# A fourth sine product moved from GpSimd to VectorE, with a new periodic order, in a software-pipelined transformer kernel

## The chip, the cores and the metric

The kernel runs on one core of a Trainium2 chip. The metric is device time in microseconds of one execution. The kernel before took 1717.99 us, the median of three runs that lay between 1716.4 and 1719.74 us.

## The reference

Two stages. First a small cross attention between `x` and `ctx` (16 batch rows of 128 tokens by 128 features). Then a six-layer network over the same 16 rows, each layer a local attention and a gated feed-forward part. The second stage takes nearly all the time:

```python
def attn_layer(x, Wqkv, qs, ksc, Wo):            # x is shift_tokens(x), 16 heads of 64
    q, k, v = split(x @ Wqkv)                    # 128 -> 3 x 1024
    q = l2norm(q) * qs; k = l2norm(k) * ksc
    q = q*cos*scale + rotate_half(q)*sin*scale   # the cosine product plus the sine product
    k = k*cos/scale + rotate_half(k)*sin/scale
    out = local_attention(q, k, v)               # windows of 32, look back one window
    return out @ Wo
def ffn_layer(x, g, bln, W1, b1, W2, b2):
    a, gate = split((layernorm(x)*g + bln) @ W1 + b1)
    return a * gelu(gate) @ W2 + b2
for i in range(6):
    x = attn_layer(shift_tokens(x), ...) + x
    x = ffn_layer(shift_tokens(x), ...) + x
```

## The kernel before, in words

One step n is one batch row in one layer; there are N = 96 of them (6 layers by 16 rows, layers outermost). A row's next layer is 16 steps later, so the steps in flight are independent, and the kernel is software-pipelined: each engine runs one loop, and iteration `it` of it works on steps it, it-1, it-2, ... at once. The number behind an operation is its lag: `scores(0, 1)` in iteration `it` works on step it-1. The order of the operations within an iteration is written out by hand for each engine (`step`, one for each of TensorE = PE, VectorE = DVE, ScalarE = ACT, GpSimd = POOL), and the engines meet only through semaphores. An engine's instructions start in order, so a waiting one holds back all that is behind it. `LAST` is the greatest lag: the loop has N + LAST iterations, the first and last of which hold only part of the work. SyncE (SP) issues the DMAs in an order of its own.

What a step does, with the lag it has before: transpose x (`turn_x`), cast it into two parts (`x_parts`, `x_rest`); four chunks of q and k of 512 columns each, by three matmuls each (`chunk`, lines 987 to 989); for each chunk the squares (ACT, line 538) and their sums by head (DVE `squares`, line 781), the cosine product (DVE `straight`, line 790) and the sine product with the halves of each head swapped. The sine product of chunks 0 to 2 is made by DVE out of PSUM (`swapped`, line 799). That of chunk 3 goes another way: ACT copies the raw chunk out of PSUM (`raw_copy`, line 544), and POOL makes the product (`swapped`, line 382). POOL adds the two products (`add`, line 390) and multiplies by the inverse norm (`normalise`, line 405); PE transposes the result (`turn_qk`, line 994, tile `u`), ACT copies it (`queries`, `keys`). Then scores (lines 1027, 1037), maxima, exponentials, `row_sums`, `divide` (POOL, line 412), `turn_p` (PE, line 994, tile `P`), `p_out` (ACT, line 594), a DMA of the turned weights into block form (`weights_of`, line 325, tile `Pbd`), and the weighted sums (`values`, line 1059), which also read the values moved by one window (`shifted_values`, line 331, tile `vs`). Then `project_out` (line 1071), `residual`, `moments` and `normal` (layer norm; ACT's `deviation`, line 609, lies between the last two), `turn_normal`, two products `up` with the next weights (342 columns), `bias`, `gelu` with two table loads, `gated`, `turn_h` (line 1100), `down` (line 1110), `feed_back`.

In the first 5 layers the weights of the next layer are split into two parts, one block in every second iteration: by ACT (`split_high`) and POOL (`split_low`, line 365). So every second iteration up to about step 80 carries one more instruction on each of the two.

The eight PSUM banks are each shared by two to four kinds of tiles (`BANK_USERS`); before PE writes a bank it waits for all readers of what stood there (`freed`, `FREED`).

Of the kernel before, what the change touches and what calls it, by code (L numbers as in the profile page):

```python
# [6 lines left out]
N = L * NB  # L7
HEADS, DH, WINDOW = 16, 64, 32
# [17 lines left out]
LAST = 4  # L26
SPLIT_LAG = 0
FINISH_AT = [N, N + 1, N + 2, N - 1 + 4]
SWAP_IN_SBUF = (3,)
# [7 lines left out]
def program(nc, x, ctxT, Wqkv, Wo, W1, b1, W2, b2, by_feature, every_token, shape_consts, out):  # L37
# [11 lines left out]
    with es:  # L49
# [43 lines left out]
        raw = sb("raw", [128, 512])  # L93
# [43 lines left out]
        def sems(name, n):  # L137
# [24 lines left out]
        xsh_ready, raw_ready, lv_done, rstd_ready, gelu_done, hT_ready, xfh_done, high_ready = (  # L162
            sem(s) for s in ("xsh_ready", "raw_ready", "lv_done", "rstd_ready", "gelu_done", "hT_ready", "xfh_done",
                             "high_ready"))
        ACT_SEMS = (sq_done + v_ready + q_ready + k_ready + exp_done + PT_ready + OT_ready + ln_done + rn_ready
                    + [xsh_ready, raw_ready, lv_done, rstd_ready, gelu_done, hT_ready, xfh_done, high_ready])
# [6 lines left out]
        xf_read = gv_full[0]  # L173
# [15 lines left out]
        def pipeline(eng, step):  # L189
# [15 lines left out]
            for it in range(tail, N + LAST):  # L205
                peeled(it)

        FREED = {"chunk": ((0, 0, 0, 0), lambda k: [sq_done[k], rot_done[k], raw_ready if k in SWAP_IN_SBUF else t2_done[k]]),
# [3 lines left out]
                 "values": ((2, 3), lambda k: [OT_ready[k]]), "up": ((4, 3), lambda k: [gv_out[k]]),  # L212
                 "Wo": ((3,), lambda k: [res_done]), "xs": ((3,), lambda k: [xh_ready]),
                 "xhT": ((3,), lambda k: [xf_done]), "turn_h": ((4,), lambda k: [hT_ready]),
                 "down": ((4,), lambda k: [h_ready]), "xT": ((0,), lambda k: [xs_split])}
        BANK_USERS = [
            [("turn_qk", 1), ("chunk", 2), ("up", 1)],
            [("xT", 0), ("Wo", 0), ("turn_p", 0), ("xhT", 0)],
            [("v", 0), ("chunk", 3)],
            [("turn_qk", 0), ("chunk", 1), ("scores", 1)],  # L220
            [("chunk", 0), ("turn_qk", 2), ("v", 1)],
            [("xs", 0), ("values", 0)],
            [("values", 1), ("scores", 0), ("turn_p", 1)],
            [("up", 0), ("turn_qk", 3), ("turn_h", 0), ("down", 0)]]
# [54 lines left out]
        def _(sp):  # L279
# [77 lines left out]
        def _(pool):  # L357
# [10 lines left out]
            def step(it, par, on, splitting):  # L368
# [7 lines left out]

                def swapped(c, lag):
                    n = it - lag
                    pool.wait_ge(raw_ready, n_(n) + 1)
                    pool.wait_ge(add_done[(c + 2) % 4], n_(n) + (c >= 2))  # L380
                    pool.sem_inc(wait_met, 1)
                    nc.gpsimd.tensor_tensor(halves(t2[:, c % 2]), halves(raw[:])[:, :, ::-1, :],
                                            TS[:, layer(n), c % 2].broadcast_to([128, HC, DH]).rearrange(
                                                "p h (a d) -> p h a d", a=2), ALU.mult).then_inc(t2_done[c], 1)
# [40 lines left out]
                if on(1):  # L425
                    normalise(1, 1)
                if on(0):
                    copy_x(0)
                if on(1):
                    add(2, 1)  # L430
                    swapped(3, 1)
                    bound_norms(1, 1)
                if splitting and (par + SPLIT_LAG) % 2 == 1:
                    split_low()
                if on(1):
                    add(3, 1)
                    normalise(2, 1)
                    normalise(3, 1)
                if on(2):
                    divide(0, 2)  # L440
                if on(4):
                    gated(4)
                if on(2):
                    divide(1, 2)
                if on(0):
                    add(1, 0)
                    bound_norms(0, 0)
                    add(0, 0)
                    normalise(0, 0)
# [773 lines left out]
```

## Time and profile before

| | |
|---|---|
| median of three runs | 1717.99 us |
| the profiled execution's own time | 1719.63 us |
| its span | 1717.8 us |
| busy PE / DVE / ACT / POOL | 1641.1 / 1467.8 / 1541.2 / 1403.3 us (96 / 85 / 90 / 82%) |
| granted TensorE clock, mean | 0.985 |

Busy time of an engine is the union of its instructions' times. A matmul's recorded end overlaps the next one's start, so a PE that is busy all the time may still lose a few tenths of a microsecond between two starts; that has to be read from the distance of starts. In the chain of waits each piece is the time by which it moved the end forward, so pieces of one engine can be added.

### The profile page before, as it was taken

To read this page: it belongs to the slowest core of one execution; us is meant where nothing else is said; L and a number is where in the kernel's file an instruction comes from. 1 tells how busy PE (TensorE), PEld (TensorE's weight loads), DVE (VectorE), ACT (ScalarE), POOL (GpSimd) and SP (SyncE) were. 2 spreads that over 40 slices of the span, in tenths; PEclk is the share of its full clock that TensorE was granted. 3 is DMA by queue.
4 is the path that set the end of the run, shared out by engine and by line. 5 is a ranking of instruction groups with operands and counts; after the bars stand their busy time and mean duration, and the time that the engine had idled before them with its cause. 6 is when DMAs were issued, how large, how long until landed. Compare 5 with 4: busy or idle time off the path is not lost.

```text
span 1717.8 us, 64013 instructions
## 1 busy us (share of the span) xinstructions
PE 1641.1 (96%) x20016; PEld 1390.2 (81%) x20016; DVE 1467.8 (85%) x3219; ACT 1541.2 (90%) x3285; POOL 1403.3 (82%) x1502
## 2 busy tenths in 40 slices
PE   4489999999999999999999999999999999999996
PEld 2368888888888888888888888888888888888885
DVE  4578888888888888888888888888889889888884
ACT  3379999999999999999999999999999999999995
POOL 1388888888888888888888888888888888888882
PEclk8699999999999999999999999999999999999999
DMA  5012322122322222222222322222232212222122
GB/s 140 23 38 66 87 61 70 49 76 54 88 58 66 63 55 75 76 67 55 69 61 58 75 73 70 54 69 57 61 91 57 64 44 64 50 57 57 49 64 59
DMA packets 71323, 110.42 MB, mean 64 GB/s; under 512 B 9716, under 2 KB 36472, under 8 KB 71288
## 3 DMA queue, kind: packets, MB, share of 16 engines
q1 hardware_dynamic: 71288, 110.01, 25.4%
q8 instruction: 15, 0.25, 0.1%
q14 instruction: 20, 0.16, 0.0%
HBM read 20.85 MB, written 1.05 MB: 13 GB/s over the span
## 4 chain that ended last, share of the span: by engine, by line
PE 42%; ACT 18%; issue 17%; DVE 8%; POOL 7%; ACTq 1%; POOLq 1%; DVEq 1%; DMA 1%; SPq 0%
PE bank L1059 7%; PE bank L994 7%; PE bank L987 6%; PE bank L989 5%; PE bank L988 5%; PE bank L1037 5%; POOL u L390 3%; ACT L620 3%; ACT kT L575 3%; POOL P L412 2%; PE bank L1110 2%; PE bank L1071 2%; ACT qbd L567 2%; ACT L623 2%; ACT P L588 2%
## 5 line engine op out<-in xcount | busy, mean ns | idle before, releaser
L390 POOL TENSOR_TENSOR u<-u,t 128x512 f32<-128x512 f32 x384 | 493.6, 1285 | 22.2 <-DVE u L790 21.6
L405 POOL TENSOR_TENSOR u<-u,rn 128x512 f32<-128x512 f32 x384 | 393.1, 1045 | 85.6 <-ACT rn L557 80.0
L987 PE MATMUL bank<-Wl,xsh 128*128 (+1 forms) x576 | 270.2, 469 | 3.5 <-issue 2.0
L790 DVE TENSOR_TENSOR u<-bank,TC 128x512 f32<-128x512 f32 x384 | 260.8, 679 | 3.4 <-ACT sq L538 3.4
L781 DVE TENSOR_REDUCE ss<-sq 128x8 f32<-128x512 f32 x384 | 259.9, 677 | 3.7 <-ACT sq L538 0.7
L1037 PEld LDWEIGHTS bank<-kT,qbd 128*64 128x64 f32 x6144 | 195.2, 138 | 61.2 <-issue 61.2
L538 ACT ACTIVATE sq<-bank 128x512 f32<-128x512 f32 x384 | 230.3, 600 | 15.4 <-PE bank L989 6.0
L567 ACT COPY qbd<-bank 64x512 f32<-64x512 f32 x384 | 222.9, 581 | 11.1 <-PE bank L994 7.7
L989 PE MATMUL bank<-Wh,xsh 128*128 (+1 forms) x576 | 228.9, 397 | 0.0
L988 PE MATMUL bank<-Wh,xsl 128*128 (+1 forms) x576 | 226.9, 394 | 0.0
L994 PE MATMUL bank<-shape_constants,u 128*128 128x128 f32 x1536 | 225.1, 278 | 0.0
L1037 PE MATMUL bank<-kT,qbd 128*64 128x64 f32 (+1 forms) x6144 | 221.7, 225 | 0.5 <-ACT kT L575 0.4
L799 DVE TENSOR_TENSOR t<-bank,TS 128x512 f32<-128x512 f32 x288 | 197.0, 684 | 18.6 <-issue 8.5
L412 POOL TENSOR_TENSOR P<-P,rs 128x512 f32<-128x512 f32 x192 | 200.9, 1047 | 10.3 <-DVE rs L820 10.3
L1059 PE MATMUL bank<-Pbd,vs 128*64 128x64 f32 x3072 | 198.8, 228 | 2.6 <-DMA Pbd<-PT 2.6
L994 PEld LDWEIGHTS bank<-shape_constants,u 128*128 128x128 f32 x1536 | 177.5, 141 | 26.3 <-issue 0.2
L1071 PEld LDWEIGHTS bank<-WB,OT 128*128 128x128 f32 x1536 | 186.1, 191 | 10.8 <-issue 2.7
L1059 PE MATMUL bank<-Pbd,v 128*64 128x64 f32 x3072 | 189.5, 222 | 0.0
L1071 PE MATMUL bank<-WB,OT 128*128 (+1 forms) x1536 | 187.1, 274 | 2.3 <-ACT OT L600 2.3
L1059 PEld LDWEIGHTS bank<-Pbd,vs 128*64 128x64 f32 x3072 | 154.8, 137 | 31.2 <-issue 16.8
L1059 PEld LDWEIGHTS bank<-Pbd,v 128*64 128x64 f32 x3072 | 155.8, 138 | 0.0
L399 POOL TENSOR_SCALAR ssc<-ss 128x16 f32<-128x16 f32 x192 | 47.6, 248 | 109.9 <-DVE ss L781 109.8
(118 smaller groups left out, 3862.6 us busy)
## 6 DMA issues: line engine op xcount, KB each, us to landing
Pbd<-PT SPq DMA_DIRECT2D x384, 128.0 KB, 2.3
vs<-v SPq DMA_DIRECT2D x96, 384.0 KB, 3.3
Wraw<-in_L_ffn_Wqkv_dram SPq DMA_DIRECT2D x72, 117.5 KB, 2.2
WB<-in_L_ffn_Wo_dram SPq DMA_DIRECT2D x6, 512.0 KB
WB<-in_L_ffn_b_dram SPq DMA_DIRECT2D x6, 341.0 KB
Wraw<-in_L_ffn_W_dram SPq DMA_DIRECT2D x12, 116.0 KB, 2.3
H<-in_x_dram SPq DMA_DIRECT2D x2, 512.0 KB, 5.6
v<-in_ctx_dram SPq DMA_DIRECT2D x2, 512.0 KB, 6.9
```

The lines of the kernel that those rows point to most:

```text
L390: nc.gpsimd.tensor_tensor(u[:, slot, c], u[:, slot, c], t2[:, c % 2], ALU.add).then_inc(add_done[c], 1)
L405: nc.gpsimd.tensor_tensor(by_head(u[:, slot, c]), by_head(u[:, slot, c]), spread(rn[:, slot, HC * c:HC * c + HC], HC, DH), ALU.mult).then_ ...
L567: i = nc.scalar.copy(qbd[r, s, :, :, e], bank_of("turn_qk", 2 * s)[r].rearrange("p (t w i) -> p t w i", t=4, w=4))
L781: nc.vector.tensor_reduce(ss[:, slot, HC * c:HC * c + HC], by_head(sq[:, c % 2]), AX, ALU.add).then_inc(ss_done[c], 1)
L790: nc.vector.tensor_tensor(by_head(u[:, slot, c]), by_head(bank_of("chunk", c)[:]), TC[:, layer(n), c % 2].broadcast_to([128, HC, DH]), ALU ...
L987: nc.tensor.matmul(out, xh_, Wl[:, w], start=True, stop=False)
L988: nc.tensor.matmul(out, xl_, Wh[:, w], start=False, stop=False)
L989: nc.tensor.matmul(out, xh_, Wh[:, w], start=False, stop=True).then_inc(done, 1)
L994: i = nc.tensor.transpose(bank[:, 128 * t:128 * t + 128], src(t), ident[:])
L1037: i = nc.tensor.matmul(out[64 * w2:64 * w2 + 64, at + (32 if w == 0 else 0):at + 64], qbd[:, s, t, w].rearrange("p e i -> p (e i)"), kT[:, ...
L1059: i = nc.tensor.matmul(tokens[64 * e:64 * e + 64, :, w2], (vs, v)[w2][:, slot, head:head + DH], Pbd[:, :, s, t, 64 * w2 + 32 * e:64 * w2 + ...
L1071: i = nc.tensor.matmul(bank_of("Wo")[:, 0:D], OT[:, k // 4, k % 4], weights(n, WO_AT + k * D, D), start=(k == 0), stop=(k == INNER // 128 ...
```

## The change

The sine product of chunk 3 is made by DVE like the other three. `raw_copy`, the tile `raw`, its semaphore, and POOL's `swapped` are gone, and so is the wait of `straight(3)` for the raw copy. The order of all engines within an iteration is written anew, with other lags for some operations: `values(0)` moves from lag 2 to 3; `deviation`, `normal`, `turn_normal`, `affine`, `upper_x`, `lower_x`, `up(1)` and `bias(1)` from 3 to 4; `gated`, `turn_h`, `h_out`, `down` and `feed_back` from 4 to 5; `minus_maxima(0)` and `exp` from 1 to 2; `normalise(1)` from 1 to 0; `shifted_values` from 2 to 1. `LAST` becomes 5. The banks are shared out anew.

```diff
-LAST = 4
+LAST = 5
-FINISH_AT = [N, N + 1, N + 2, N - 1 + 4]
-SWAP_IN_SBUF = (3,)
+FINISH_AT = [N, N + 1, N + 2, N - 1 + 5]
...
-        FREED = {"chunk": ((0, 0, 0, 0), lambda k: [sq_done[k], rot_done[k], raw_ready if k in SWAP_IN_SBUF else t2_done[k]]),
+        FREED = {"chunk": ((0, 0, 0, 0), lambda k: [sq_done[k], rot_done[k], t2_done[k]]),
...
-            [("turn_qk", 1), ("chunk", 2), ("up", 1)],
-            [("xT", 0), ("Wo", 0), ("turn_p", 0), ("xhT", 0)],
...
+            [("values", 1), ("xhT", 0), ("turn_qk", 3), ("Wo", 0), ("up", 1)],
+            [("turn_qk", 1), ("v", 0), ("turn_p", 0)],
...
+            [("xT", 0), ("chunk", 0), ("chunk", 3)]]
...
                 if 0 <= it - 2 < N:
-                    shifted_values(it - 2)
-                if 0 <= it - 2 < N:
                     weights_of(it - 2, 0)
+                if 0 <= it - 1 < N:
+                    shifted_values(it - 1)
                 if 0 <= it - 2 < N:
                     weights_of(it - 2, 1)
...
-                def swapped(c, lag):
-                    n = it - lag
-                    pool.wait_ge(raw_ready, n_(n) + 1)
-                    pool.wait_ge(add_done[(c + 2) % 4], n_(n) + (c >= 2))
-                    pool.sem_inc(wait_met, 1)
-                    nc.gpsimd.tensor_tensor(halves(t2[:, c % 2]), halves(raw[:])[:, :, ::-1, :],
...
-                def raw_copy(c, lag):
-                    n = it - lag
-                    act.wait_ge(ch_full[c], n_(n) + 1)
-                    act.wait_ge(t2_done[c], n_(n))
-                    nc.scalar.copy(raw[:], bank_of("chunk", c)[:]).then_inc(raw_ready, 1)
...
                 def straight(c, lag):
                     n, slot = it - lag, (par + lag) % 2
                     dve.wait_ge(sq_done[c], n_(n) + 1)
-                    if c in SWAP_IN_SBUF:
-                        dve.wait_ge(raw_ready, n_(n) + 1)
```

How the orders of an iteration differ is read from the built programs. TensorE around the transposes of the attention weights (`P`), before:

```order
L994 MATMUL bank_4<-shape_constants,u 128x128 x4
L994 MATMUL bank_7<-shape_constants,u 128x128 x4
L1079 MATMUL bank_5<-H,shape_constants 128x64
L994 MATMUL bank_1<-shape_constants,P 128x128 x4
L987 MATMUL bank_0<-Wl,xsh 128x512
L988 MATMUL bank_0<-Wh,xsl 128x512
L989 MATMUL bank_0<-Wh,xsh 128x512
```

and now (line 972 is the transpose, 1049 `project_out`, 965 to 967 a product, 1005 the start of `scores`):

```order
L972 MATMUL bank_6<-shape_constants,u 128x128 x4
L1049 MATMUL bank_0<-WB,OT 128x128 x8
L972 MATMUL bank_1<-shape_constants,P 128x128 x4
L965 MATMUL bank_3<-Wl,xfh 128x342
L966 MATMUL bank_3<-Wh,xfl 128x342
L967 MATMUL bank_3<-Wh,xfh 128x342
L972 MATMUL bank_6<-shape_constants,P 128x128 x4
L1005 MATMUL bank_4<-maskb,identb 128x512
```

`turn_p(0)` stood right behind `shift`; now it stands behind `project_out`, in the last third of the iteration, and the values that it leads to are the second operation on TensorE in the next one.

VectorE in the last part of an iteration, before (tile `t2` is the sine product, `u` the cosine product):

```order
L849 TENSOR_SCALAR xh<-bank_5,mv,rstd 128x64
L790 TENSOR_TENSOR u<-bank_0,TC 128x512
L806 TENSOR_REDUCE nm<-bank_3 128x8
L812 TENSOR_TENSOR P<-bank_3,nm 128x512
L857 TENSOR_SCALAR xf<-bank_1,feature_columns 128x128
L799 TENSOR_TENSOR t2<-bank_0,TS 128x512
L864 TENSOR_TENSOR xfl<-xf,xfh 128x128
L781 TENSOR_REDUCE ss<-sq 128x8
L790 TENSOR_TENSOR u<-bank_2,TC 128x512
L871 TENSOR_TENSOR value<-bank_0,WB 128x341
```

and now:

```order
L848 TENSOR_TENSOR gate<-bank_3,WB 128x341
L760 TENSOR_REDUCE ss<-sq 128x8
L776 TENSOR_TENSOR t2<-bank_7,TS 128x512
L760 TENSOR_REDUCE ss<-sq 128x8
L783 TENSOR_REDUCE nm<-bank_4 128x8
L810 BN_STATS bst<-H 128x6
L812 BN_STATS bst<-bank_6 128x6
L816 BN_AGGR mv<-bst 128x2
L789 TENSOR_TENSOR P<-bank_4,nm 128x512
L848 TENSOR_TENSOR value<-bank_0,WB 128x341
L783 TENSOR_REDUCE nm<-bank_5 128x8
```

The row `t2<-bank_7` is the added product. `normal` (`xh`), which stood one instruction behind the moments that it needs (`mv`), is now in the next iteration.

SyncE, before (two DMAs for each half of the attention weights):

```order
L331 DMA vs<-v 96x1024
L325 DMA Pbd<-PT 64x512 x4
L331 DMA vs<-v 96x1024
L325 DMA Pbd<-PT 64x512 x4
L331 DMA vs<-v 96x1024
```

and now:

```order
L323 DMA Pbd<-PT 64x512 x4
L329 DMA vs<-v 96x1024
L323 DMA Pbd<-PT 64x512 x4
L329 DMA vs<-v 96x1024
L323 DMA Pbd<-PT 64x512 x2
```

The DMA of the moved values, which went ahead of both halves, now stands between the first and the second half.

## Rows read from the trace of the kernel before

**Rows 1.** Windows: stretch, length, busy PE, PEld, DVE, ACT, POOL, clock, DMA

```profile
73.00:132.00 59.00, 45.65 (x456) 35.40 (x457) 42.73 (x82) 37.24 (x85) 45.72 (x50) 0.86 0.13 33
132.00:1405.00 1273.00, 1266.31 (x15728) 1079.13 (x15727) 1130.89 (x2432) 1201.46 (x2545) 1105.57 (x1178) 1.00 0.26 66
1405.00:1671.00 266.00, 266.00 (x3314) 226.18 (x3312) 236.67 (x513) 248.81 (x529) 223.76 (x240) 1.00 0.22 56
1671.00:1718.00 47.00, 31.12 (x380) 26.14 (x378) 20.71 (x54) 27.54 (x51) 12.51 (x14) 0.93 0.24 63
```

**Rows 2.** Line 531, first and last start: whole span, 200:1380, 1405:1640

```profile
L531 ACT CAST xsh<-bank x96: 252/259/266, 74.0 to 1654.9; 64x128 fp32r<-64x128 f32 x96
...
L531 ACT CAST xsh<-bank x70: 259/259/266, 215.2 to 1371.9; 64x128 fp32r<-64x128 f32 x70
...
L531 ACT CAST xsh<-bank x15: 259/259/265, 1405.5 to 1638.3; 64x128 fp32r<-64x128 f32 x15
```

**Rows 3.** The chain of waits at 1421.85 to 1438.48: start, length, what

```profile
1421.85 0.11 PE bank L1001
...
1422.88 1.08 PE bank L1059 x32
...
1425.97 1.78 PE bank L1071 x16
1427.76 0.22 PE bank L1027
1427.97 1.08 PE bank L1037 x32
1429.06 1.02 PE bank L994 x8
...
1432.09 0.48 PE bank L1100 x3
...
1438.37 0.11 PE bank L1001
```

**Rows 4.** TensorE's timeline at 826.60: start, length, instruction, idle before

```profile
826.60 0.33 PE L1079 MATMUL bank<-H,shape_constants 128*128 x2
827.11 0.66 PE L994 MATMUL bank<-shape_constants,P 128*128 128x128 f32 x4 [0.18 <-POOL P L412]
```

**Rows 5.** GpSimd's timeline before the same place

```profile
821.62 1.21 POOL L365 TENSOR_TENSOR Wl<-Wraw,Wh  x1 [0.49 <-issue]
...
826.01 1.04 POOL L412 TENSOR_TENSOR P<-P,rs 128x512 f32<-128x512 f32 x1
```

**Rows 6.** The groups of instructions by line: busy us, mean ns, idle before

```profile
L799 DVE TENSOR_TENSOR t<-bank,TS 128x512 f32<-128x512 f32 x288 | 197.0, 684 | 18.6 <-issue 8.5 <-ACT sq L538 4.4 <-POOL u L390 1.0
...
L382 POOL TENSOR_TENSOR t<-raw,TS 128x512 f32<-128x512 f32 x96 | 124.6, 1298 | 0.0
L620 ACT ACT_TABLE_LOAD x96 | 123.2, 1283 | 1.7
...
L544 ACT COPY raw<-bank 128x512 f32<-128x512 f32 x96 | 55.6, 579 | 0.0
```

**Rows 7.** The waits in 200:1380: total us, times, longest

```profile
DVE xh L847 <- ACT rstd L609: 49.6, 70, 0.9
```

**Rows 8.** VectorE's timeline at 1443.81

```profile
1443.81 0.68 DVE L790 TENSOR_TENSOR u<-bank,TC 128x512 f32<-128x512 f32 x1
1444.40 0.68 DVE L781 TENSOR_REDUCE ss<-sq 128x8 f32<-128x512 f32 x1
```

**Rows 9.** The page's DMA issues: KB each, us to landing

```profile
Pbd<-PT SPq DMA_DIRECT2D x384, 128.0 KB, 2.3
vs<-v SPq DMA_DIRECT2D x96, 384.0 KB, 3.3
```

**Rows 10.** The chain of waits in the drain

```profile
1712.24 1.63 PE bank L1110 x6
...
1714.33 0.75 DVE X L934
```

More of the change, by code:

```diff
@@ L429, in step @@
                 if on(1):
+                    bound_norms(1, 1)
+                    add(3, 1)
                     add(2, 1)
-                    swapped(3, 1)
-                    bound_norms(1, 1)
+                if on(5):
+                    gated(5)
                 if splitting and (par + SPLIT_LAG) % 2 == 1:
@@ L881, in step @@
                     x_rest(0)
-                if on(1):
-                    squares(2, 1)
+                if on(2):
+                    minus_maxima(0, 2)
+                if on(4):
+                    normal(4)
                 if on(2):
                     row_sums(1, 2)
+                if on(0):
+                    swapped(0, 0)
+                    straight(0, 0)
                 if on(4):
-                    bias(0, 4)
+                    affine(4)
                 if on(2):
@@ L890, in step @@
                 if on(0):
-                    swapped(0, 0)
-                    straight(0, 0)
                     squares(1, 0)
                     swapped(1, 0)
+                    squares(0, 0)
+                if on(5):
+                    feed_back(5)
+                if on(0):
+                    straight(3, 0)
+                if on(4):
+                    lower_x(4)
+                if on(0):
+                    straight(1, 0)
+                    swapped(2, 0)
                 if on(3):
@@ L1115, in step @@
                     turn_x(0)
-                if on(4):
-                    up(0, 4)
+                if on(1):
+                    turn_qk(1, 1)
+                if on(3):
+                    values(0, 3)
                 if on(1):
@@ L1124, in step @@
                 if on(1):
-                    turn_qk(1, 1)
+                    v_chunk(0, 1)
                 if on(0):
                     chunk(1, 0)
-                if on(3):
-                    project_out(3)
-                if on(1):
-                    scores(0, 1)
-                    turn_qk(2, 1)
-                    turn_qk(3, 1)
-                if on(3):
-                    shift(3)
-                if on(2):
-                    turn_p(0, 2)
+                if on(5):
+                    turn_h(5)
+                if on(4):
+                    turn_normal(4)
                 if on(0):
@@ L1140, in step @@
                 if on(1):
-                    v_chunk(0, 1)
+                    v_chunk(1, 1)
+                    turn_qk(3, 1)
+                if on(0):
+                    chunk(3, 0)
+                if on(5):
+                    down(5)
+                if on(1):
+                    turn_qk(2, 1)
+                if on(3):
+                    project_out(3)
+                if on(2):
+                    turn_p(0, 2)
                 if on(4):
-                    turn_h(4)
+                    up(0, 4)
+                if on(2):
+                    turn_p(1, 2)
                 if on(1):
                     scores(1, 1)
-                if on(2):
-                    turn_p(1, 2)
-                if on(0):
-                    chunk(3, 0)
                 if on(3):
-                    turn_normal(3)
+                    shift(3)
+                if on(4):
+                    up(1, 4)
                 if on(1):
-                    v_chunk(1, 1)
-                if on(4):
-                    down(4)
-                if on(2):
-                    values(0, 2)
-                if on(3):
-                    up(1, 3)
+                    scores(0, 1)
             pipeline(pe, step)
```

126 lines of the change are left out of this document (52 added, 74 removed).

## The prediction

> **What bounds the kernel now.** I read the windows view first, stage by stage. Between 132 and 1671 us TensorE is busy 99.5 and 100% of the time [rows 1]; ACT has 1201 of 1273 us, DVE 1131, POOL 1106. So the kernel is bound by TensorE, or by waits so short that the overlapping ends of matmuls hide them. The busy share can't tell these apart; the distance of starts can. Line 531 runs once in each iteration. From 215.2 to 1371.9 there are 69 distances: 16.76 us each. From 1405.5 to 1638.3 there are 14: 16.63 us each [rows 2]. The first stretch has the split of the next layer's weights in every second iteration, the second has not. The instructions of TensorE are the same in both, so at least 0.13 us of 16.76 are no TensorE work.
>
> Then I read the chain of waits over one iteration of the second stretch. All of its pieces are TensorE's, from 1421.85 to 1438.37: 16.52 us [rows 3]. One piece is too long for its work: three transposes at line 1100 take 0.48, while eight at line 994 of the same shape take 1.02, 0.13 each, which include entering from small tiles; plain ones would be 0.33 to 0.38. So 0.10 to 0.15 is a wait (for `hh`, from POOL). That puts TensorE's own work at 16.37 to 16.42 us. The next iteration starts the same way but lasts longer, since two of them make 2 x 16.63 = 33.26 and one has 16.52: the other has 16.74, another 0.2 of wait.
>
> Then TensorE's timeline in the first stretch. Two small matmuls start at 826.60, and the transpose of P behind them at 827.11, 0.51 later; the two themselves take 0.33 with their overlapping end. The view shows 0.18 us of idle time, ended by `divide` on POOL; counted between starts nearer 0.3 are lost [rows 4]. POOL's own rows say why: at 821.62 it starts the split, 1.21 us, and five instructions later `divide` ends at 827.05, just before TensorE goes on [rows 5]. This happens in every second iteration. So what TensorE waits for now is POOL, behind the split. Together the four waits (0.3 at P and 0.1 around it in one iteration, 0.13 and 0.2 in the other, halved) are some 0.35 to 0.4 us an iteration, and 16.76 - 0.4 = 16.36, which agrees with the floor from rows 3.
>
> **The change part by part.** *POOL* loses 96 products of 1.30 us [rows 6]. Its busy time in an iteration, 1105.57/1273 x 16.76 = 14.6 us [rows 1], falls to 13.3. The split's 1.21 then fits into 3 us of slack, and in the new order `divide(0)` is followed on TensorE's side by a turn that comes after `project_out` (1.78 [rows 3]) and not right after `shift`. Taking off the wait at P is worth 0.15 to 0.2 an iteration as a mean, the one at line 1100 (`turn_h`, now of lag 5, with its inputs made an iteration earlier) 0.07 to 0.15.
>
> *ACT* loses 96 copies of 0.58 us [rows 6]: from 1201.46/1273 x 16.76 = 15.8 to 15.3 us. It was the second fullest engine; it has now 1.1 us of slack to a period of 16.4.
>
> *DVE* gains 96 products. The three like it that it makes already take 0.684 us [rows 6], and starts of such instructions that follow each other are 0.59 to 0.60 apart (1443.81, 1444.40 [rows 8]). The added one so costs 0.60 to 0.68. DVE has 1130.89/1273 x 16.76 = 14.9 busy, so 15.5 to 15.6 now. Its idle time of 1.9 us holds one large piece, `normal` waiting for ACT's `rstd`: 49.6 us in 70 iterations, 0.71 each [rows 7] (0.9 in the second stretch). In the new order `normal` is an iteration later and that wait is gone. So 16.63 - 0.9 + 0.6 = 16.3 if every other gap stayed: DVE just fits under TensorE's floor, with nothing to spare on this reckoning. Most of its other gaps (before `bias` and `x_rest`) are waits for TensorE that would shrink, so I take DVE's own need as 16.0 to 16.3. At nothing I cost the product's latency: the sum of the two products goes to POOL in the next iteration, behind `copy_x` and `bound_norms`, and what covers it is POOL's 3 us; if it did not, turning chunk 3 on TensorE is some 7 us into the iteration.
>
> The Trainium skill, in "VectorE: DVE Perf Modes", section on the TRN2 errata, charges a VectorE operation out of PSUM 120 cycles beside its elements against 58 out of SBUF (658 against 594 ns at 512 elements, an estimate from its table), and its rules for kernel authors advise a copy to SBUF where many operations follow: both speak against giving up the raw copy. The trace does not show the difference: product out of PSUM 0.68, sum of squares out of SBUF 0.68 [rows 8]. By the page's difference the change would lose 0.06 us an iteration on DVE, which is not the bound.
>
> *Banks.* Chunk 3's bank is now read by ACT, then DVE twice, and is next written by the x transpose at the start of the next iteration. The added product stands ten instructions before the end on DVE, some 2 us before that. I cost it at nothing; it would cost what DVE is late beyond 2 us.
>
> *TensorE's order.* No instruction is added. One of the two ways from the small-tile `values` into a product becomes one into a transpose. Price between -0.06 and +0.05 an iteration, taken as 0.
>
> *SP and DMA.* The second half of the turned weights is now issued behind the moved values. From the end of `turn_p(1)` to `values(1)` TensorE has two `scores` (2 x (0.22 + 1.08)), two turns of q or k (2 x 0.51), and one `values` (1.08) [rows 3], 4.7 us, and with `up`, `shift` and the x transpose, which have no row here, about 5.7. In that time must come the norms and a copy on ACT (1.1), the issues (two of about half a microsecond) and the landing, 2.3 [rows 9]: 4.4. If the landing is as late as that of the moved values in front, 3.3 [rows 9], it is 5.4. So 0.3 to 1.3 us to spare, if ACT is on time. I take no wait.
>
> *Period.* Floor 16.36. I add 0.07 in the first stretch (the split still adds 0.6 to ACT and 1.2 to POOL in every other iteration, against slack of 1.1 and 3) and 0.02 in the second: 16.43 and 16.38. Bounds: 16.30 (the transitions come out better) and 16.76 (nothing is won).
>
> *Ends.* Iteration 80 starts at 1405.5; counting back by 16.76, iteration 4 starts at 131.4, so iterations 0 to 3 take 57.4 us for their work in part, because each is bound by latency (TensorE is busy 45.65 of 59 us [rows 1]). Now iteration 4 is incomplete as well, but misses only `turn_h` and `down` of TensorE's work: it takes about what a full one does, -0.5 us. At the end batch 95 passes through one more iteration. Its chain of operations is as long as before, but two things now stand in its way: `feed_back` of the step before is ahead of `lower_x` on DVE, and waits for `down` (1.63 in the drain [rows 10]); and ACT's second table load (1.28 [rows 6]) is ahead of `deviation`. I take +3.5 us for both, between 0 and 6. The last piece, the sum with X and the store from 1714.33 on, stays.
>
> *Sum.* First stretch, 75 iterations: 75 x (16.76 - 16.43) = -24.8. Second, 16 iterations: 16 x (16.63 - 16.38) = -4.0. Fill -0.5, drain +3.5. Total -25.8 us. Against the profiled execution's own time, 1719.6, that is 1693.8. This execution is 1.6 above the median of the runs, 1718.0; against the median it is 1692.
>
> **The rivals.**
>
> *DVE or ACT becomes the bound.* DVE then has a period of its own of 16.5 to 16.7: the added 0.60 to 0.68 in full, and the gaps stay. For it: the reckoning 16.3 had no slack, and its sine and cosine products wait for ACT's squares, and after each such wait everything behind on DVE is late. Against it: the chunk products are consumed late. At 16.6 the first stretch gives 75 x 0.16 = -12, the second -0.5, the ends +3: 1708.
>
> *Nothing is recovered.* The waits at TensorE move but stay as long: 16.76 and 16.63, and the ends +3: 1721. For it: several things end at nearly the same time there. Against it: POOL is relieved of 1.3 us on the very path that TensorE waits for.
>
> *Slower: `values` waits for its DMA.* The place is `values(1)`, second half; the mechanism is the moved values' DMA, 384 KB, issued just before the 128 KB that `values(1)` needs, with ACT's `p_out(1)` late behind `norms(0)`. It decides from the point where the landing is later than the 0.3 to 1.3 us to spare. A landing 1 us later than that costs 16.36 + 1.0 = 17.4 in every iteration at worst; with half of it, 16.9, the stretch loses 75 x 0.14 = 10 and 16 x 0.27 = 4: with the ends 1735. Break-even is a wait of 0.37. For it: 3.3 against 2.3 in rows 9. Against it: the turned weights' wait on SP is now the long one, and TensorE waits for no such DMA today.
> The Trainium skill, "DMA: Bandwidth & Descriptors", section on queues, rings and completion order, says that on each DMA engine descriptors of one ring are taken in ring order. By that the 128 KB must queue behind the 384 KB, and this rival is more than a guess; no row here shows the two that close together.
>
> **How the numbers follow.** A time within 0.2% (3.4 us) of 1718.0 can't be told from no change. The forecast, period 16.3 to 16.5, has 0.60: 1682 to 1700. DVE or ACT as bound 0.21: 1700 to 1716. Nothing recovered 0.07, 1716 to 1722. Slower 0.12: 1722 to 1745. The range that holds 8 in 10 goes from 1681 to 1717. Faster by over 0.2%: 0.60 + 0.20 = 0.80; within 0.2%: 0.06; slower: 0.14.
>
> **What the new profile would show.** Right: starts of `x_parts` 16.4 apart in both stretches, with 0.05 or less between them; the chain of waits made of TensorE pieces in the first stretch too; no wait of a transpose of P for POOL; DVE busy 15.5 to 15.6 an iteration, no `xh` waiting for `rstd`; POOL's idle time up by 1.3. Wrong: a wait of TensorE's `values` for `Pbd`, a chain that runs along DVE from iteration to iteration, or a drain more than 6 us longer than the 62.9 us from 1654.9 [rows 2] to the end.

## The result, and the profile after

The changed kernel took 1707.04 us, the median of four runs from 1706.97 to 1708.74, beside 1718.45 for the kernel before on the same chip (four runs, 1716.40 to 1719.74). The ratio is 0.9937, with a 95% interval from 0.992 to 0.9954: faster by 11.4 us, where 26 were forecast. A repeat on another chip gave 0.9917 [0.9903, 0.993]. The profiled execution took 1706.97 us of its own, with a span of 1705.1.

The page of the kernel after: the span, the engines, the shares of the chain of waits, the costliest group of sine products, and the two DMAs (KB, median us to landing).

```profile
span 1705.1 us, 63781 instructions
...
PE 1630.9 (96%) x20016; PEld 1396.9 (82%) x20016; DVE 1504.3 (88%) x3315; ACT 1514.4 (89%) x3189; POOL 1274.7 (75%) x1406
...
PE 89%; DMA 2%; ACT 1%; issue 1%; SPq 1%; DVE 1%; POOL 0%; POOLq 0%; DVEq 0%; ACTq 0%
...
L776 DVE TENSOR_TENSOR t<-bank,TS 128x512 f32<-128x512 f32 x384 | 262.7, 684 | 63.3 <-ACT sq L524 63.3
...
Pbd<-PT SPq DMA_DIRECT2D x384, 128.0 KB, 3.1
...
vs<-v SPq DMA_DIRECT2D x96, 384.0 KB, 3.5
```

TensorE now holds 89% of the chain: outside the two ends hardly anything but TensorE's own pieces sets the time. The product out of PSUM still takes 684 ns, 384 of them instead of the 288 of [rows 6]. The 128 KB DMA has a median of 3.1 us to landing instead of 2.3 [rows 9]. That median mixes two kinds: those of the first half of the weights still land in 2.24 and 2.36 us, those of the second half, issued 0.6 and 1.2 us behind the 384 KB, in 3.41 and 3.29 (medians in 200:1380).

The windows of the same stages, columns as in [rows 1]:

```profile
73.00:131.00 58.00, 44.35 (x448) 35.06 (x450) 43.12 (x81) 35.40 (x80) 42.19 (x48) 0.86 0.13 36
131.00:1390.00 1259.00, 1255.53 (x15707) 1080.71 (x15704) 1153.64 (x2505) 1177.64 (x2466) 1002.50 (x1102) 1.00 0.26 67
1390.00:1655.00 265.00, 264.26 (x3327) 228.76 (x3325) 247.50 (x530) 245.59 (x513) 202.44 (x224) 1.00 0.21 56
1655.00:1705.00 50.00, 34.31 (x409) 28.74 (x405) 22.89 (x59) 29.62 (x55) 11.93 (x12) 0.88 0.21 54
```

And the line that runs once in each iteration (517 now, 531 in [rows 2]), over the whole span, over 200:1380, and over the end of the second stage:

```profile
L517 ACT CAST xsh<-bank x96: 258/258/261, 73.0 to 1638.4; 64x128 fp32r<-64x128 f32 x96
...
L517 ACT CAST xsh<-bank x71: 258/258/261, 215.5 to 1373.9; 64x128 fp32r<-64x128 f32 x71
...
L517 ACT CAST xsh<-bank x13: 258/258/260, 1440.2 to 1638.4; 64x128 fp32r<-64x128 f32 x13
```

1158.4 / 70 = 16.55 us from start to start in the first stretch, and 198.2 / 12 = 16.52 in the last part of the second. With the starts of iterations 5 and 80 (148.2 and 1405.5 before, 147.9 and 1389.9 now) the span divides into four parts:

| part | before | after | forecast for after |
|---|---|---|---|
| start of iteration 5 | 148.2 | 147.9 | 147.7 |
| iterations 5 to 80, each | 16.764 | 16.560 | 16.43 |
| iterations 80 to 95, each | 16.63 | 16.57 | 16.38 |
| last start to the end | 62.9 | 66.7 | 66.2 |

The forecast span was 1717.8 - 25.8 = 1692.0; the measured one is 13.1 longer. Of these, 9.5 lie in the 75 iterations of the first stretch (0.13 each), 2.8 in the 15 of the second (0.19 each), and 0.7 in the ends. So the error is in the period. The 3.8 us more at the end agree with the 3.5 of the forecast (66.2 in the table is 62.9 + 3.5, less the one period of the sum that ends behind the last start).

The waits of 200:1380 (total us, times, longest), the one that is longest in total and TensorE's only one:

```profile
POOL P L401 <- DVE rs L797: 126.9, 107, 2.1
...
PE bank L1037 <- DMA Pbd<-PT: 0.4, 1, 0.4
```

The wait of TensorE for `divide` is gone, and so is that of `xh` for `rstd` [rows 7]. GpSimd is the one that waits now, 1.8 us an iteration before `divide`; it is no longer late. What TensorE still loses stands in its chain, here around two entries into `up(0)`, which is line 965 behind the transpose of P:

```profile
821.31 0.44 PE bank L972 x4
821.75 0.33 PE bank L965
...
832.04 0.33 PE bank L1078 x3
...
837.88 0.44 PE bank L972 x4
838.32 0.16 PE bank L965
```

The three transposes at line 1078 (1100 before) take 0.33 instead of 0.48 [rows 3]. But the same matmul at line 965 takes 0.33 in one iteration and 0.16 in the next. The view of waits shows nothing there, and the chain gives it to TensorE itself. The program's order tells the two apart; the loop's body holds two iterations, one for each parity (ISA and REGISTER_ALU are instructions of TensorE's queue):

```
L972 MATMUL bank_1<-shape_constants,P 128x128 x4
L965 ISA
L965 MATMUL bank_3<-Wl,xfh 128x342
...
L972 MATMUL bank_1<-shape_constants,P 128x128 x4
L965 ISA
L965 REGISTER_ALU
L965 MATMUL bank_3<-Wl,xfh 128x342
```

TensorE's queue works out where in `Wl` and `Wh` the layer's weights lie (`(b // NB) % 2 * W_SPLIT_SIZE`), and one parity has a step more. That is one half of the reading, and it is tested below. The other half is a wait for VectorE. `up(0)` goes into the bank of chunk 1, and the last to read chunk 1 is VectorE's cosine product, `straight(1)`. In the late iteration:

```profile
820.45 0.69 DVE L767 TENSOR_TENSOR u<-bank,TC 128x512 f32<-128x512 f32 x1
821.68 0.40 PE L965 MATMUL bank<-Wl,xfh 128*128 x1
```

The trace also has the rows of TensorE's queue, which the views leave out. The row that waits for the semaphore of `straight(1)` stands 0.04 us behind the end of `straight(1)` in every iteration of 200:1380 (here 821.17 behind 821.13), so the queue waits for VectorE there each time. The address comes behind it: a register row of 148 ns and one more in the late parity, one of 60 ns in the other. The product starts 0.55 us after the end of `straight(1)`, too late for the end of the transposes in one parity. So the 0.17 us are a wait and an address one behind the other.

### The profile page after: what moved, and what is told of

The parts are those of the page before. It is cut to its first block, busy times and chain, and to the rows that moved or that the text cites. A ratio compares the mean times of both kernels' runs of the same rounds, so it can differ in the third digit from the quotient of the medians.

```text
span 1705.1 us, 63781 instructions
## 1 busy us (share of the span) xinstructions
PE 1630.9 (96%) x20016; PEld 1396.9 (82%) x20016; DVE 1504.3 (88%) x3315; ACT 1514.4 (89%) x3189; POOL 1274.7 (75%) x1406
## 4 chain that ended last, share of the span: by engine, by line
PE 89%; DMA 2%; ACT 1%; issue 1%; SPq 1%; DVE 1%; POOL 0%; POOLq 0%; DVEq 0%; ACTq 0%
PE bank L972 15%; PE bank L1037 12%; PE bank L1015 11%; PE bank L965 11%; PE bank L1049 10%; PE bank L967 9%; PE bank L966 9%; PE bank L1088 4%; PE bank L1005 2%; PE bank L1057 2%; DMA Pbd<-PT 2%; PE bank L1078 2%; PE bank L979 1%; SPq L323 1%; PE bank L1064 1%
## 5 line engine op out<-in xcount | busy, mean ns | idle before, releaser
L379 POOL TENSOR_TENSOR u<-u,t 128x512 f32<-128x512 f32 x384 | 486.1, 1276 | 102.6 <-DVE u L767 102.5
L776 DVE TENSOR_TENSOR t<-bank,TS 128x512 f32<-128x512 f32 x384 | 262.7, 684 | 63.3 <-ACT sq L524 63.3
L965 PE MATMUL bank<-Wl,xsh 128*128 (+1 forms) x576 | 254.1, 441 | 2.9 <-DVE xsl L753 2.2
L972 PE MATMUL bank<-shape_constants,u 128*128 128x128 f32 x1536 | 237.2, 277 | 0.0
L972 PEld LDWEIGHTS bank<-shape_constants,u 128*128 128x128 f32 x1536 | 175.6, 141 | 22.2 <-issue 6.4
L1049 PEld LDWEIGHTS bank<-WB,OT 128*128 128x128 f32 x1536 | 179.1, 192 | 0.0
L789 DVE TENSOR_TENSOR P<-bank,nm 128x512 f32<-128x512 f32 x192 | 131.0, 682 | 3.0
```

The costliest lines, as they stand in the source:

```text
L379: nc.gpsimd.tensor_tensor(u[:, slot, c], u[:, slot, c], t2[:, c % 2], ALU.add).then_inc(add_done[c], 1)
L776: nc.vector.tensor_tensor(halves(t2[:, c % 2]), halves(bank_of("chunk", c)[:])[:, :, ::-1, :], TS[:, layer(n), c % 2].broadcast_to([128, H ...
L965: nc.tensor.matmul(out, xh_, Wl[:, w], start=True, stop=False)
L972: i = nc.tensor.transpose(bank[:, 128 * t:128 * t + 128], src(t), ident[:])
L1049: i = nc.tensor.matmul(bank_of("Wo")[:, 0:D], OT[:, k // 4, k % 4], weights(n, WO_AT + k * D, D), start=(k == 0), stop=(k == INNER // 128 ...
```

## The experiments

The first four (e1 to e4) ran on one chip, beside a before of 1720.76 (median of 27); the next four (e5 to e8) on another, before 1719.72 (median of 9); the last four (e9 to e12) on a third, before 1722.29 (median of 17). All ratios are to the kernel before. "Period" is iterations 5 to 80, then 80 to 95. The period of the second stretch is the rougher figure: it has 15 iterations, and code that an edit leaves alone there differs by up to 0.07 from one execution to another (16.63 in the kernel before, 16.70 in e3).

### The edit without the order: e1_swap_old_order

```diff
-SWAP_IN_SBUF = (3,)
+SWAP_IN_SBUF = ()
-                    swapped(3, 1)      # POOL
-                    raw_copy(3, 0)     # ACT
+                    swapped(3, 0)      # DVE, behind straight(3, 0)
```

> The sine product of chunk 3 on VectorE (behind straight(3)), no raw copy, but the old order, lags and banks. Theory A (the edit alone takes POOL's 1.3 us off the path on which TensorE waits for it): the period falls to about 16.63 in both stretches, 1705 to 1712 us. Theory B (the edit needs the new order, because in the old one VectorE still waits 0.7 to 0.9 us for rstd behind its own moments and has no room for 0.6 more): VectorE becomes the bound, period 16.9 to 17.2, 1725 to 1760 us.

1723.76 us, 1.0016 [1.0002, 1.003]; period 16.81 and 16.76. Neither theory holds whole: the edit alone gains nothing, and it does not cost what theory B expected either (16.9 to 17.2). Its waits in 200:1380:

```profile
POOL ssc L399 <- DVE ss L779: 175.6, 70, 2.6
...
PE bank L993 <- POOL P L412: 6.2, 35, 0.2
```

GpSimd spends its freed 1.3 us waiting for DVE's sums of squares: 175.6 us where the kernel before has 83.0. `divide` comes no earlier, and TensorE waits for it 35 times, as before.

### The order without the edit: e2_new_order_raw and e12_new_order_raw_dma_last

```diff
+    raw_copy(3, 0)     # ACT, behind square(3, 0), in the new order
+    swapped(3, 1)      # POOL, ahead of add(3, 1)
-    swapped(3, 0)      # DVE
```

> The new order, lags and banks, but chunk 3's sine product on POOL again from a raw copy by ACT (raw_copy behind square(3), POOL's swapped ahead of add(3)). Theory A (what pays is the order, which TensorE follows at its own pace): period 16.5 to 16.6, 1705 to 1712 us. Theory B (what pays is the relief of ACT and POOL): waits for POOL or ACT come back in the iterations with the split, period 16.7 or more, 1717 us or more.

1726.98 us, 1.0037 [1.0025, 1.005]; period 16.76 and 16.60; 69.9 us from the last start to the end. The new order alone loses: 6 us against the kernel before, most of them in the ends, since the period is the old one. To see whether the order of the DMAs is what costs it, e12 is the same kernel with the moved values issued behind both halves of the weights (the edit of e7 below).

> e2 (the new order with chunk 3's sine product still on POOL behind ACT's raw copy) with the moved values' DMA last. Theory A (e2's loss of 17 us against the changed kernel is that p_out(1) on ACT came late before a DMA with no slack): it falls to 1708 to 1712 us. Theory B (the loss is ACT's and POOL's own load): 1720 or more.

1722.9 us, 1.0009 [1.0001, 1.0018], as theory B had it; the period stays at 16.76 and 16.60. The DMA order was 4 us of ends; the loop's loss is another. The window 200:1380 and waits in it, of VectorE and of TensorE:

```profile
200.00:1380.00 1180.00, 1170.47 (x14531) 1003.47 (x14529) 1019.67 (x2251) 1119.69 (x2360) 1019.84 (x1091) 1.00 0.26 65
```
```profile
DVE xsl L771 <- ACT xsh L530: 54.8, 70, 1.1
...
DVE u L788 <- ACT raw L542: 11.8, 46, 0.3
...
PE bank L985 <- issue: 9.5, 35, 0.3
```

ACT has 15.9 of 16.76 us. DVE waits for its cast of x in every iteration (54.8 us in 70; in the changed kernel 20.1 in 36), and `straight(3)` for the raw copy, 11.8 us in 46 times. Line 985 is the first line of every product; the one that waits is `up(0)` again. Its queue row stands 0.04 us behind the end of `straight(1)`, as in the changed kernel, but `straight(1)` itself ends later: from the last transpose of P to `up(0)` it takes 0.55 us in one iteration and 0.18 in the other, where e7, the same kernel with the product on VectorE, has 0.21 and 0.03. That is 0.24 us a mean iteration, all of the difference between 16.76 and e7's 16.53. In the second stretch, which has no split, the period is 16.60. So the order needs `straight(1)` on time, and ACT's raw copy and late cast push it back; how much each of the two does is not separated.

### The kernels without the split: e3_before_nosplit and e4_after_nosplit

```diff
-    split_low()        # POOL, every second iteration
-    split_high()       # ACT
+    # both weight halves are filled once, ahead of the loop
```

> The kernel before without the split of the next layers' weights in the loop (ACT's and POOL's one instruction in every second iteration; the layers after the first read constants, so this part of the computation is left out). If the old kernel loses its time to POOL behind the split, every iteration takes the 16.63 us of its second stretch: 76 x 0.13 = 10 us less, 1708 us. If not, no change, 1718 us.

> The changed kernel without the split in the loop (the same part left out). If TensorE's own stream, with what its sequencer prepares, is the bound in both stretches, little is left to gain: period 16.49, 2 to 4 us less, 1703 to 1705 us. If the 0.13 us an iteration that the forecast was short are waits behind the split, the period falls to 16.38 and the time to 1692 to 1695 us.

e3 took 1711.57 us, 0.9951 [0.9937, 0.9964]; e4 1710.48, 0.9944 [0.9926, 0.9963]. Both start 3 us later, for the fill. Line 529 of e3 and line 515 of e4:

```profile
L529 ACT CAST xsh<-bank x71: 259/260/265, 201.8 to 1363.5; 64x128 fp32r<-64x128 f32 x71
```
```profile
L515 ACT CAST xsh<-bank x72: 258/258/261, 204.1 to 1377.5; 64x128 fp32r<-64x128 f32 x72
```

1161.7 / 70 = 16.60 and 1173.4 / 71 = 16.53. Without the split the kernel before gains 0.17 an iteration and the changed one 0.02 (iterations 5 to 80: 16.60 and 16.54). So three quarters of the change's 0.20 (0.17 - 0.02) is the cost of the split, which the changed kernel hides. What stays between the two orders without it is 0.05 to 0.07. e3 gained more than the 0.13 that was expected; e4 is at neither of its two expectations (16.49 and 16.38), and in time it gains nothing on the changed kernel. Neither is a kernel without waits: e3 still waits at line 1100, e4 at `up(0)` and `values(1)`, as the account below shows.

### One instruction moved in the kernel before: e11_before_split_late

```diff
     # POOL: split_low() stood ahead of divide(1, 2)
+    divide(1, 2)
     split_low()
```

> The kernel before with one thing moved: POOL's split_low goes behind divide(1, 2), so that it no longer delays the divide that TensorE's turn_p waits for. Theory A (this wait was what the split costs, 0.17 us a mean iteration): period 16.76 to 16.60, 12 us less, 1706 to 1709 us. Theory B (the split costs through ACT, or the delay only moves to the next thing POOL makes, the added products of chunks 0 and 1): 1714 to 1720 us.

1712.5 us, 0.9945 [0.9933, 0.9958]. Window and line 531:

```profile
200.00:1380.00 1180.00, 1180.00 (x14661) 1002.76 (x14660) 1053.49 (x2268) 1115.65 (x2374) 1031.14 (x1099) 1.00 0.26 66
```
```profile
L531 ACT CAST xsh<-bank x71: 258/258/270, 200.6 to 1365.8; 64x128 fp32r<-64x128 f32 x71
```

TensorE is busy for all of the 1180 us, and 1165.2 / 70 = 16.65. The wait that was read in [rows 4, 5] was POOL behind the split, and taking it off by itself gives 0.12 of the 0.20 us that the whole change gives. That lies between the two theories (0.16 and nothing). The reason is in the distances of starts: the iteration with POOL's split loses all 0.50 us at and around P, but gets 0.16 at line 1100, which the wait at P had covered; the other gets 0.09 more, nearly all at `up(0)`. Half of 0.50 - 0.16 - 0.09 is 0.12.

### A constant address: e6_before_fixed_up and e5_after_fixed_up

```diff
-    w = ds((b // NB) % 2 * W_SPLIT_SIZE + at, size)
+    w = slice(at, at + size) if fixed else ds((b // NB) % 2 * W_SPLIT_SIZE + at, size)
...
-    product(..., gv_full[k])
+    product(..., gv_full[k], fixed=(k == 0))      # up(0) alone
```

> The kernel before without the split, up(0) at a constant address too. Theory S: the 0.2 us between turn_x and up(0) in every second iteration falls to 0.03, period of e3 less 0.08, some 7 us less than e3. That would say that this part of what the forecast took for a wait was the sequencer's. Theory W: as e3.

> The changed kernel without the split, and up(0) reads its weights at a constant address instead of one that TensorE's sequencer computes from the step (numbers of another layer, so this part is left out). Theory S (the 0.17 us between turn_p(0) and up(0) in every second iteration is the sequencer computing the address, with nothing long ahead of it to cover it): that distance falls from 0.17 to 0.03, the period by 0.07, some 6 us less than e4. Theory W (it is a wait for VectorE, for the bank of chunk 1 or for xfl): distance and time as in e4.

e6 (e3 with this edit) took 1704.84 us, 0.9914 [0.9899, 0.9929]: period 16.53 where e3 has 16.60. TensorE's timeline at the way from the transpose of x into `up(0)`, first e3, then e6, the same parity:

```profile
831.82 0.27 PE L999 MATMUL bank<-shape_constants,xw 128*128 128x128 f32 x1
831.96 0.43 PE L985 MATMUL bank<-Wl,xfh 128*128 x1
```
```profile
828.22 0.27 PE L999 MATMUL bank<-shape_constants,xw 128*128 128x128 f32 x1
828.25 0.40 PE L985 MATMUL bank<-Wl,xfh 128*128 128x342 f32 x1
```

0.14 from start to start becomes 0.03. In the other parity e3 has 0.03 too (815.29 to 815.32). That is the fourth wait of the forecast, the one of "another 0.2": it was no wait for an engine. It was TensorE's queue and its registers. Here no wait stands in front: the rows of the queue follow each other without a gap, and in this parity the loop's branch (0.21 us) comes just ahead of them.

e5 (e4 with this edit) took 1709.79, 0.9936 [0.9921, 0.9951]: period 16.53 and 16.56, only 0.013 less than e4. The gap behind the transpose of P is gone (0.03 in both parities), but this is, in e5, the next product that needs the address, `up(1)` behind `shift`, in two neighbouring iterations:

```profile
826.77 0.43 PE L1055 MATMUL bank<-H,shape_constants 128*128 x2
827.10 0.39 PE L963 MATMUL bank<-Wl,xfh 128*128 x1
...
843.24 0.43 PE L1055 MATMUL bank<-H,shape_constants 128*128 x2
843.48 0.40 PE L963 MATMUL bank<-Wl,xfh 128*128 x1
```

0.33 against 0.24; in e4 it is 0.24 and 0.25. The address is computed where it is first used, and it is in the open there too. In e6 nothing came back: the period fell by 0.066, where 0.11 in every second iteration is 0.055 as a mean.

### The DMA of the moved values last: e7_values_dma_last

```diff
                     weights_of(it - 2, 0)
-                if 0 <= it - 1 < N:
-                    shifted_values(it - 1)
                 if 0 <= it - 2 < N:
                     weights_of(it - 2, 1)
+                if 0 <= it - 1 < N:
+                    shifted_values(it - 1)
```

> The changed kernel with shifted_values issued behind both halves of the weights and not between them. Theory D (values(1) waits up to 0.13 us in every second iteration since its DMA lands behind the moved values'): the median landing of the turned weights goes from 3.1 back to 2.3 to 2.6, the waits of values vanish, period 16.56 to 16.50, 3 to 5 us less than the changed kernel, 1702 to 1704. Theory R (the landing is covered): no change, 1707 us.

1700.04 us (1699.24 to 1701.54), 0.9885 [0.987, 0.99], span 1698.1: more than the 3 to 5 us that theory D gave. Its 128 KB DMA, its line 517, and the start of the second `values`; then the last of the changed kernel:

```profile
Pbd<-PT SPq DMA_DIRECT2D x384, 128.0 KB, 2.3
```
```profile
L517 ACT CAST xsh<-bank x71: 258/258/260, 212.4 to 1369.8; 64x128 fp32r<-64x128 f32 x71
```
```profile
840.82 0.66 PE L972 MATMUL bank<-shape_constants,u 128*128 128x128 f32 x4
841.41 0.34 PE L1037 MATMUL bank<-Pbd,vs 128*64 128x64 f32 x4
```
```profile
844.44 0.66 PE L972 MATMUL bank<-shape_constants,u 128*128 128x128 f32 x4
845.12 0.34 PE L1037 MATMUL bank<-Pbd,vs 128*64 128x64 f32 x4
```

The landing is back at 2.3 us. The step into `values(1)` takes 0.59 there, in the changed kernel 0.68 in this iteration and 0.59 in the one before it: a wait that the view of waits hides under the overlapping ends. As a mean of 200:1380 that step is 0.269 in every second iteration, 0.202 in the others and 0.202 throughout in e7: 0.03 an iteration. By parts: the first start 0.4 earlier, 1.3 less to iteration 5, 75 x 0.032 = 2.4, 15 x 0.06 = 0.9, and 1.9 at the end (64.8): 6.9 of the 7.0 us between the spans. The first of these is no more than two executions of one kernel differ by (73.0 and 74.9 in the changed kernel). The drain shows it best. The chain of the changed kernel, then of e7:

```profile
1666.65 0.54 SPq L329
...
1667.28 0.56 SPq L323
...
1667.89 3.23 DMA Pbd<-PT
...
1671.16 1.18 PE bank L1037 x32
```
```profile
1671.86 0.55 SPq L323
...
1672.46 2.43 DMA Pbd<-PT
...
1674.93 1.18 PE bank L1037 x32
```

The issue of the 384 KB (0.54 at line 329) and 0.8 of longer landing are gone from the path. The trace agrees with the rule of the Trainium skill that the prediction weighed ("DMA: Bandwidth & Descriptors", queues, rings and completion order): the second half's 128 KB land in 3.41 and 3.29 us behind the 384 KB, and in 2.31 and 2.35 ahead of it. Transfers that share the same engines at the same time would look alike; no run tells the two apart.

### `feed_back` behind `lower_x`: e8_feed_back_late and e10_dma_last_feed_back_late

```diff
     # DVE
-    feed_back(5)
     lower_x(4)
+    feed_back(5)
```

> The changed kernel with feed_back(5) behind lower_x(4) on VectorE. In the drain lower_x of the last batch then doesn't wait for down of the one before: by the forecast's reckoning up to 2 us less there (66.7 from the last start of x_parts to the end, now 64.7 or more), the period as it is; 1705 to 1707 us. If the period grows, VectorE has less room than taken.

1705.62 us (1702.93 to 1708.96), 0.9912 [0.9898, 0.9925]. The profile does not show the gain that was to come: from the last start to the end it has 70.1 us, more than the 66.7 of the changed kernel. A window in its drain, and the product at line 1049 in its chain:

```profile
1675.00:1681.00 6.00, 5.23 (x29) 5.01 (x28) 1.23 (x4) 1.46 (x3) 0.33 (x1) 0.67 0.01 3
```
```profile
1674.91 3.41 PE bank L1049 x16
```

3.41 us where the changed kernel's chain has 1.79 for the same sixteen, at a granted clock of 0.67 in that window, which is part at the level of 1.2 and part at 2.4 GHz. The profiled execution is the slowest of its five, and its total of 1705.62 can't be told from the changed kernel's (0.9912 and 0.9917). One profile with the lower level in another place can't say what the move itself is worth. Both edits together:

> The changed kernel with both edits of e7 (the moved values' DMA last) and e8 (feed_back behind lower_x). If they are independent: the period of e7, 16.53, and a drain no longer than 64.8 us: 0.9865 to 0.989 of the kernel before. If feed_back does not count in the drain, as e8 suggests, the same as e7 alone, 0.9885.

1702.12 us, 0.9883 [0.9869, 0.9898], span 1702.9, 65.8 at the end, where 64.8 or less was expected; the profiled execution is the slowest of its four. Its period is 16.56 and 16.46, not the 16.53 of e7: the wait at `values(1)` is gone here too, but `up(0)` and another product in the late iteration take 0.02 more each. By the ratio that is e7 (0.9885), so no gain of the move of `feed_back` is shown.

The chains of the drain do show the mechanism that was forecast. In the changed kernel:

```profile
1692.34 0.92 PE bank L1088 x6
...
1693.60 0.29 DVE xfl L841
...
1693.93 0.66 PE bank L965
```

From the end of `down` (line 1088) through `feed_back` (855) and `lower_x` (841) to the next product it takes 0.67 us, and 0.68 in e7. In e8 and e10 the product follows `down` at once. But `down` itself takes 1.62 us in both, at the lower clock, and that takes the gain back.

### The changed kernel again: e9_after_again

> The changed kernel as it is, so that the other three stand beside it on one chip: 0.9937 of the kernel before, within 0.15%.

1708.28 us, 0.9917 [0.9903, 0.993], period 16.57 and 16.60. The ratio is 0.2% under the expected 0.9937, so ratios taken on different chips can differ by that much for one kernel. On the same chip e10 is 1708.28 - 1702.12 = 6.2 us faster. e7 and e10 both beat the two kernels.

## Why the prediction was right in direction and wrong in size

*Right.* The bound was read rightly: TensorE, held up by POOL behind the split. The parts shown after agree. The wait at P is gone, the one of `xh` for `rstd` too, line 1078 takes 0.33, the two stretches differ by 0.01, the chain is TensorE's. POOL's idle time rose from 2.2 to 3.4 us an iteration, by 1.2 (forecast 1.3). VectorE's price for a product out of PSUM, on which the trace and the Trainium skill's "VectorE: DVE Perf Modes" differed, decided nothing, since VectorE did not become the bound.

*Where 16.56 comes from.* Every iteration of 200:1380 has all of its 208 matmuls in the trace, so the distances of starts can be averaged place by place, for each parity. The table has the two iterations of the loop's body, the excess over the usual distance at the few places that have any, and what is left without it, in us:

| kernel | slower / other iteration | excess in the slower one | excess in the other | both without it |
|---|---|---|---|---|
| before | 16.86 / 16.66 | at and around P 0.50 | line 1100 0.15, `up(0)` 0.13 | 16.36 / 16.37 |
| e3 | 16.67 / 16.52 | line 1100 0.15, `up(0)` 0.14 | line 1100 0.15 | 16.37 / 16.37 |
| e6 | 16.53 / 16.53 | line 1100 0.15 | line 1100 0.15 | 16.37 / 16.37 |
| changed | 16.67 / 16.43 | `up(0)` 0.17, `values(1)` 0.07 | none | 16.44 / 16.43 |
| e4 | 16.62 / 16.43 | `up(0)` 0.13, `values(1)` 0.07 | none | 16.43 / 16.43 |

The 16.36 of the forecast was therefore a right figure for the old order. No run had it as its pace, but three kernels come down to it.

*The steps that failed, all in the period.* The first is "TensorE's order ... taken as 0": an iteration of the new order without any excess takes 16.43, so the new sequence of the same matmuls costs 0.06 to 0.07, a little over the bound of 0.05. The second is that all of the 0.4 of waits were counted as won. Of the four, the two at P were POOL's, and the new order takes them off. The one at line 1100 is gone too, but it was not for `hh`: `turn_h` shares its bank with the turned chunk 3, and its transposes start 0.14 us after ACT's copy of that chunk (`keys`) ends, in all 35 waits of the trace of before; the row of TensorE's queue for that copy's semaphore stands 0.04 us behind its end. Two rows of one of them:

```profile
811.35 0.59 ACT L575 COPY kT<-bank 128x512 f32<-128x512 f32 x1
...
812.08 0.52 PE L1100 MATMUL bank<-shape_constants,hh 128*128 128x128 f32 x3
```

The fourth, "another 0.2 of wait", was TensorE's queue working out an address (e6: 0.14 falls to 0.03, the period by 0.066), and relief of POOL does nothing for it. The new order puts that address behind a wait for VectorE's `straight(1)`, where 0.17 stands in the open in every second iteration, 0.08 as a mean. The third is "I take no wait" for `values(1)`: 0.03 as a mean. 16.43 + 0.08 + 0.03 = 16.54 to 16.55, against 16.55 to 16.56 measured. The 0.07 that the forecast allowed for the split, of which e4 shows 0.02, happens to be as large as the cost of the new sequence; that its 16.43 is also the clean iteration is luck.

These excesses are not prizes to be added. With the address made constant at `up(0)`, e5 has 16.53 where e4 has 16.54; the DMA order gives 0.03 in e7, and in e10 that 0.03 comes back at other places (16.56).

*The drain* came out 3.8 us longer (forecast 3.5), and the agreement is in part luck. 1.9 is the DMA order (e7), which was not in that term. 0.7 is `feed_back` in front of `lower_x`, the reason that was given. The table load ahead of `deviation`, the other reason, is not on the chain. Most of the rest is the clock: the granted level falls to 1.2 GHz 12.0 us before the end in the changed kernel, and 6.4 before it in the kernel before. Two products and three transposes of the last chain then take 1.23, 0.87 and 0.92 us, where the kernel before has 0.75 for a first product, 0.47 for one behind another and 0.56 for the transposes: some 1.2 us, an estimate from these rows.

*DVE or ACT as the bound* (1708 by its sum) gave nearly the measured time and is still not what happened: a kernel bound by DVE would not have 89% of its chain on TensorE. A part of its mechanism is there, though: one product of VectorE, `straight(1)`, is what `up(0)` waits for. DVE's busy time rose only to 1153.64 / 1259 x 16.56 = 15.2 us, where 15.5 to 15.6 were forecast. That is not because the product is cheap. In 200:1380 it adds 0.50 us an iteration in the old order (14.89 before, 15.39 in e1) and 0.70 in the new one (14.48 in e12, 15.18 in e7); but the new order alone takes 0.4 off (14.89 to 14.48).

*`values` waiting for its DMA* was the right mechanism in the wrong size: it is there, with 0.03 us an iteration as a mean rather than the 1 us that its price took. The spare time was put at 0.3 to 1.3 us. There is none, by a little.

*Nothing recovered* describes e1 and e12, and e2 with 4 us more in its ends. The change's gain is in neither part alone. The order needs VectorE's `straight(1)` free of the raw copy and of ACT's late cast, and the edit needs `divide` out of the way of DVE's sums.

## What to carry to other kernels

An excess between two starts on the bounding engine can be a wait for an engine, work of its own queue, or both in a row, as at `up(0)`. Look for a neighbour's row that ends at a constant distance before it, and at what the queue has to do between the two, register arithmetic for an address above all, and in which parity. Waits cover each other, so several of them are worth less than their sum: taking off 0.50 us at P uncovered 0.25 elsewhere (e11). Before adding them up, measure a cheap variant: the kernel before without the split (e3) would have put the forecast at 1718 - 75 x 0.17 + 3 = 1708. And a new order has a pace of its own, which rows of the old one do not give. When one relief is needed, move the one instruction that is in the way first; it gave over half of what 96 removed products and a new order gave.

## What the runs showed of the hardware

- Address arithmetic on TensorE's queue came into the open in one parity of two: 0.14 us behind the x transpose in e3 (0.03 in the other parity), and 0.17 in the changed kernel, there behind a wait for VectorE. Made constant at its first use, it came back at the second by 0.09 (e5).
- The row of TensorE's queue that waits for `straight(1)` stood 0.04 us behind that instruction's end, and the product 0.55 behind it with the address to be worked out, 0.41 with a constant one (e5, where it no longer held the product up).
- A DMA of 128 KB issued 0.6 to 1.2 us behind one of 384 KB landed in 3.3 to 3.4 us, ahead of it in 2.2 to 2.4.
- A product of 128 x 512 out of PSUM on DVE takes 684 ns in its row; it added 0.50 us to the engine's busy time in the old order and 0.70 in the new one.
- In the drain, the same sixteen matmuls took 3.41 us in one execution and 1.79 in another, at a granted clock of 0.67 in the window around the slow ones.
